# Second stage of a three-stage decoder kernel: the probability tiles are turned by VectorE in 32x32 blocks and eight DMAs, and the values come from two full-width products

## The reference

```
Q, K, V = split_heads(layernorm(x) @ W_Q), split_heads(ctx @ W_K), split_heads(ctx @ W_V)
E = einsum('bhqd,bhkd->bhqk', Q, K)            # one 64x64 block for each sequence and head
E = where(key_padding_mask, -inf, E)
A = softmax(E / sqrt(64))
x = x + einsum('bhqk,bhkd->bhqd', A, V).reshape(b, 64, 1024) @ W_O
```

## Time and profile before

| | |
|---|---|
| median of 3 runs | 3386.17 us (3384.32 to 3388.98) |
| profiled execution, span from first to last instruction | 3389.4 us |
| PE, DVE, ACT, POOL busy over the span | 98%, 82%, 83%, 73% |
| PE matmuls in one pass of stage two | 11.02 us busy of 11.15 us |
| DVE, ACT, POOL in the same pass | 5.12, 7.05, 3.10 us busy |
| second stage, first scores of tile 0 to last products of tile 31 | 194.4 to about 564 us |

### The profile page before, as it was taken

One profiled execution on the slowest core, in us unless ns is written; L12 is line 12 of the kernel. 1 busy time (PEld: TensorE's weight loads), 2 busy tenths in 40 slices (PEclk: granted clock), 3 DMA queues, 4 the chain that ended last, 5 costly groups with the idle time before them and its releaser, 6 DMA issues.

```text
span 3389.4 us, 120739 instructions
## 1 busy us (share of the span) xinstructions
PE 3317.7 (98%) x49605; PEld 2474.5 (73%) x49605; DVE 2767.5 (82%) x5297; ACT 2803.2 (83%) x5522; POOL 2483.0 (73%) x4812
## 2 busy tenths in 40 slices
PE   8989998999999999999999999999999999999997
PEld 6777876577777777777777777777777777777776
DVE  6844445888888888888888888888888888899995
ACT  5756665688888888888888888888888888888885
POOL 4622223888888888888888888888888888888884
PEclk8999999999999999999999999999999999999999
DMA  3000001544444444445444444444444444444441
GB/s 108 3 7 9 8 9 35 102 83 84 85 91 98 94 84 82 83 94 105 88 82 83 89 94 98 85 86 83 95 102 83 85 85 92 83 89 85 89 88 41
DMA packets 200381, 260.15 MB, mean 77 GB/s; under 512 B 123161, under 2 KB 145438, under 8 KB 199838
## 3 DMA queue, kind: packets, MB, share of 16 engines
q0 software_dynamic: 55296, 201.35, 31.4%
q1 hardware_dynamic: 143820, 50.88, 6.1%
q10 hardware_dynamic: 722, 0.21, 0.0%
HBM read 23.95 MB, written 2.10 MB: 8 GB/s over the span
## 4 chain that ended last, share of the span: by engine, by line
PE 95%; DVE 2%; POOL 1%; issue 1%; DMA 1%; ACT 1%; SPq 0%; DVEq 0%; POOLq 0%
PE bank L1059 19%; PE bank L1034 17%; PE bank L1110 10%; PE bank L1187 10%; PE bank L1158 8%; PE bank L1174 6%; PE bank L1129 5%; PE bank L1051 4%; PE bank L675 2%; PE bank L1124 2%; PE bank L688 2%; PE bank L697 2%; PE bank L752 2%; PE bank L367 1%; PE bank L660 1%; PE bank L377 1%
## 5 line engine op out<-in xcount | busy, mean ns | idle before, releaser
L1348 DVE TENSOR_TENSOR R<-bank,tables 128x1024 f32<-128x1024 f32 x768 | 904.7, 1220 | 174.7 <-ACT sq L1246 167.2
L1059 PE MATMUL bank<-WA,xcT 128*128 128x512 f32 x1536 | 723.6, 593 | 3.0 <-ACT xcT L1221 2.1
L1034 PEld LDWEIGHTS bank<-ident,R 128*128 128x128 f32 x3072 | 365.0, 141 | 214.7 <-issue 201.2
L1361 DVE TENSOR_REDUCE ss<-sq 128x16 f32<-128x1024 f32 x384 | 460.1, 1198 | 0.0
L1473 POOL TENSOR_TENSOR P<-P,inv_sum 128x512 f32<-128x512 f32 x384 | 447.6, 1331 | 2.9 <-DVE inv_sum L1402 2.9
L1246 ACT ACTIVATE sq<-bank 128x512 f32<-128x512 f32 x768 | 431.3, 587 | 16.0 <-PE bank L1059 16.0
L1034 PE MATMUL bank<-ident,R 128*128 128x128 f32 x3072 | 431.2, 273 | 8.8 <-POOL R L1461 6.8
L1461 POOL TENSOR_TENSOR R<-R,rn 128x512 f32<-128x512 f32 x384 | 400.4, 1043 | 31.5 <-DMA R<-R 5.4
L1467 POOL TENSOR_TENSOR P<-P,rn 128x512 f32<-128x512 f32 x384 | 402.6, 1048 | 4.3 <-DVE P L1390 4.3
L1059 PEld LDWEIGHTS bank<-WA,xcT 128*128 128x128 f32 x1536 | 262.2, 191 | 188.9 <-issue 184.0
L1187 PE MATMUL bank<-WO,OT 128*128 128x128 f32 x3072 | 374.6, 275 | 0.0
(11 more groups left out here) (154 smaller groups left out, 6857.6 us busy)
## 6 DMA issues: line engine op xcount, KB each, us to landing
R<-R POOLq DMA_DIRECT2D x384, 512.0 KB, 5.0
WA<-in_wqkv SPq DMA_DIRECT2D x24, 256.0 KB, 2.9
ystat<-Y SPq DMA_DIRECT2D x192, 32.0 KB
ystat<-Y SPq DMA_DIRECT2D x384, 15.8 KB
ys<-Y SPq DMA_DIRECT2D x192, 32.0 KB
ys<-Y SPq DMA_DIRECT2D x384, 15.8 KB
WV<-in_wqkv SPq DMA_DIRECT2D x6, 512.0 KB, 4.0
WO<-in_wo SPq DMA_DIRECT2D x6, 512.0 KB, 4.3
```

The source lines that it names most:

```text
L1034: return nc.tensor.transpose(dst, src, m.ident[:, :])
L1059: mm(b[QK_BANK[n, half]][:, :], m.xsT[:, t % 2, :], cols[:, half, :, :], start=True, stop=True)\
L1348: tt(both, src.unsqueeze(1).to_broadcast([128, 2, 16, 32]), tab.unsqueeze(2).to_broadcast([128, 2, 16, 32]), ALU.mult).then_inc(s.rotated. ...
L1361: nc.vector.tensor_reduce(m.ss[:, t % 2, 16 * n:16 * n + 16], m.sq[:, n, :].rearrange("p (h d) -> p h d", d=HD), AX.X, ALU.add)\
```

## The change

`probs_turned` moves from TensorE to VectorE. There, two `transpose` instructions a tile, one for each half of 512 columns, turn each 32x32 block in place within its group of 32 partitions and write it to `BLOCKS`, a part of the buffer `R` that only stage three uses otherwise. A block that must change its group of partitions is then moved by DMA: SyncE issues eight DMAs a tile from `BLOCKS` to `PT`, each from 32 partitions to 32 partitions, two runs of 1 KB on each partition (64 KB). `head_outputs` waits for all eight (semaphore `p_moved`, 128 a tile), and `probs_turned` waits for those of the tile before. ScalarE's two copies `probs_out` go. `PT` now has the keys of a sequence on one half of the partitions, so the values can stand by token: `values` makes two products of 128 tokens by 512 columns each. `outputs_out` writes `OT` in another order, and the wait for `y1` goes to `out_projection`.

```diff
+    BLOCKS = m.R[:, 0, 0, :].rearrange("p (a k n) -> p a k n", a=2, k=2)
+    PT = m.PT[:, :, :].rearrange("p t (a q n) -> p t a q n", a=2, q=2)
...
     @m.sync.append
     def _(sp):
+        def probs_moved(t):
+            if exists(t):
+                sp.wait_ge(s.p_turned[1], t + 1)
+                sp.wait_ge(s.p_turned[0], t + 1)
+                for to in range(4):
+                    for q in range(2):
+                        frm = to - to % 2 + q
+                        sp.dma_start(PT[32 * to:32 * to + 32, t % 2, :, q, :], BLOCKS[32 * frm:32 * frm + 32, :, to % 2, :])\
+                            .then_inc(s.p_moved[t % 2], 16)
...
         for t in range(N):
             at_least(sp, s.x_turned, t - 3)
             sp.dma_start(m.ctx_sb[:, t % 4, :], ctx_tiles[t, :, :]).then_inc(s.ctx[t % 4], 16)
+            probs_moved(t - 2)
+        for t in range(N - 2, N):
+            probs_moved(t)
...
         def out_projection(t):
             if exists(t):
                 pe.wait_ge(s.o_copied[0], t + 1)
                 pe.wait_ge(s.o_copied[1], t + 1)
+                at_least(pe, s.y1, t)
...
-        def probs_turned(t, j):
-            if exists(t):
-                pe.wait_ge(s.normal[j], t + 1)
-                if j == 1:
-                    at_least(pe, s.y1, t)
-                for n in range(4):
-                    at = j * 512 + n * 128
-                    last = turned(PT_BANK[j][:, n * 128:(n + 1) * 128], m.P[:, t % 2, at:at + 128])
-                last.then_inc(s.p_turned[j], 1)
...
         def head_outputs(t):
             if exists(t):
-                for j in range(2):
-                    pe.wait_ge(s.v_copied[j], t + 1)
-                    pe.wait_ge(s.p_copied[j], t + 1)
...
+                pe.wait_ge(s.v_copied[0], t + 1)
+                pe.wait_ge(s.v_copied[1], t + 1)
+                pe.wait_ge(s.p_moved[t % 2], 128 * (t // 2) + 128)
...
-        def values(t, bb):
-            if exists(t):
-                cols = WV.rearrange("p (j e n) -> p e j n", e=2, n=128)
-                for e in range(2):
-                    last = mm(V_BANK[bb][64 * e:64 * e + 64, :], m.ctxT[:, t % 2, bb * 64:bb * 64 + 64],
-                              cols[:, e, :, :], start=True, stop=True)
-                last.then_inc(s.v[bb], 1)
...
+        def values(t, j):
+            if exists(t):
+                mm(V_BANK[j][:, :], m.ctxT[:, t % 2, :], WV[:, j * 512:(j + 1) * 512], start=True, stop=True)\
+                    .then_inc(s.v[j], 1)
...
-            probs_turned(i - 1, 1)
-            probs_turned(i - 1, 0)
...
-            probs_out(i - 1, 1)
-            probs_out(i - 1, 0)
...
+        def probs_turned(t, a):
+            if exists(t):
+                dve.wait_ge(s.normal[a], t + 1)
+                at_least(dve, s.p_moved[(t - 1) % 2], 128 * ((t + 1) // 2))
+                blocks = m.P[:, t % 2, a * 512:(a + 1) * 512].rearrange("p (h k n) -> p k h n", k=2, n=32)
+                nc.vector.transpose(BLOCKS[:, a, :, :].rearrange("p k (h n) -> p k h n", n=32), blocks)\
+                    .then_inc(s.p_turned[a], 1)
...
             inverse_sums(i - 1, 1)
             inverse_sums(i - 1, 0)
+            probs_turned(i - 1, 1)
+            probs_turned(i - 1, 0)
             added(i - 2)
             less_maximum(i, 1)
             less_maximum(i, 0)
```

More of the change, by code:

```diff
@@ L624, in cross_attention @@
     S_BANK, QT_BANK, KT_BANK = (b[0], b[3]), (b[1], b[2]), (b[0], b[3])
-    V_BANK, PT_BANK, PV_BANK = (b[5], b[1]), (b[6], b[7]), (b[2], b[4])
+    V_BANK, PV_BANK = (b[5], b[1]), (b[2], b[4])
     OUT, TURNED_IN = b[7], b[4]
     WQ, WK, WV, WO = m.WA[:, 1, 0:INNER], m.WA[:, 1, INNER:2 * INNER], m.cross_wv, m.WO[:, 1, :]
+    BLOCKS = m.R[:, 0, 0, :].rearrange("p (a k n) -> p a k n", a=2, k=2)
+    PT = m.PT[:, :, :].rearrange("p t (a q n) -> p t a q n", a=2, q=2)
     def pair(name):
@@ L638, in cross_attention @@
     s.row_sum, s.inverse, s.normal = pair("row_sum"), pair("inverse"), pair("normal")
-    s.p_turned, s.p_copied = pair("p_turned"), pair("p_copied")
+    s.p_turned, s.p_moved = pair("p_turned"), pair("p_moved")
     s.o, s.o_copied, s.wo, s.y1 = sem("cross_o"), pair("o_copied"), sem("cross_wo"), sem("cross_y1")
@@ L672, in out_projection @@
                 pe.wait_ge(s.o_copied[1], t + 1)
+                at_least(pe, s.y1, t)
                 for c in range(PAIRS):
-                    at = (c % 2) * 512 + c // 2 * 128
-                    last = mm(OUT[:, 0:128], m.OT[:, t % 2, at:at + 128], WO[:, c * 128:(c + 1) * 128],
+                    last = mm(OUT[:, 0:128], m.OT[:, t % 2, c * 128:c * 128 + 128], WO[:, c * 128:(c + 1) * 128],
                               start=(c == 0), stop=(c == PAIRS - 1))
@@ L733, in head_outputs @@
             if exists(t):
-                for j in range(2):
-                    pe.wait_ge(s.v_copied[j], t + 1)
-                    pe.wait_ge(s.p_copied[j], t + 1)
[L737 to L746, removed]
-        def values(t, bb):
-            if exists(t):
-                cols = WV.rearrange("p (j e n) -> p e j n", e=2, n=128)
-                for e in range(2):
-                    last = mm(V_BANK[bb][64 * e:64 * e + 64, :], m.ctxT[:, t % 2, bb * 64:bb * 64 + 64],
-                              cols[:, e, :, :], start=True, stop=True)
-                last.then_inc(s.v[bb], 1)
+                pe.wait_ge(s.v_copied[0], t + 1)
+                pe.wait_ge(s.v_copied[1], t + 1)
+                pe.wait_ge(s.p_moved[t % 2], 128 * (t // 2) + 128)
+                for hp in range(PAIRS):
+                    for bb, a in ((0, 0), (1, 1), (0, 1), (1, 0)):
+                        rows, head, vals = slice(64 * bb, 64 * bb + 64), slice(64 * a, 64 * a + 64), (2 * hp + a) * 64
+                        last = mm(PV_BANK[bb][head, hp * 64:hp * 64 + 64], m.V[rows, t % 2, vals:vals + 64],
+                                  PT[rows, t % 2, a, :, hp * 32:hp * 32 + 32], start=True, stop=True)
+                        if hp == PAIRS - 1 and (bb, a) in ((0, 1), (1, 0)):
+                            last.then_inc(s.o, 1)
+        def values(t, j):
+            if exists(t):
+                mm(V_BANK[j][:, :], m.ctxT[:, t % 2, :], WV[:, j * 512:(j + 1) * 512], start=True, stop=True)\
+                    .then_inc(s.v[j], 1)
         for i in range(N + 2):
@@ L799, in exponents @@
                 nc.scalar.activation(part, part, ACT.Exp, scale=HD ** -0.5).then_inc(s.probs[a], 1)
-        def probs_out(t, j):
-            if exists(t):
-                act.wait_ge(s.p_turned[j], t + 1)
-                copy(m.PT[:, t % 2, j * 512:(j + 1) * 512], PT_BANK[j][:, :]).then_inc(s.p_copied[j], 1)
         def outputs_out(t, e):
@@ L808, in outputs_out @@
                 act.wait_ge(s.o, 2 * t + 2)
-                copy(m.OT[:, t % 2, e * 512:(e + 1) * 512], PV_BANK[e][:, :]).then_inc(s.o_copied[e], 1)
+                copy(m.OT[:, t % 2, :].rearrange("p (c b q) -> p b c q", b=2, q=SEQ)[:, e, :, :],
+                     PV_BANK[e][:, :].rearrange("p (c q) -> p c q", q=SEQ)).then_inc(s.o_copied[e], 1)
         def normalised(t):
```

## The result

| | before | after |
|---|---|---|
| median of 4 runs (lowest to highest) | 3387.43 us (3384.32 to 3388.98) | 3460.7 us (3456.55 to 3462.52) |
| ratio, 95% interval | | 1.0217 (1.0202 to 1.0231) |

What follows compares the result with a forecast made beforehand. PE's list was taken to bound the kernel, 11.16 us a tile. Ring 1 at 11.93 gave +23.1, first period -0.2, stage end +3.3, pauses about -1: together +25 on 3386.2, forecast 3411 us, range 3400 to 3446.

Steps and rivals of the forecast that it cites:

- Slower: Whole kernel: the change makes it slower by more than 0.2%, 6.8 us; chance 0.88.
- The transpose on VectorE: Each of VectorE's two transposes a tile takes 0.69 us, bounds 0.51 and 1.20.
- Ring 1: Stage two, scores through VectorE's transposes, `added`, `Y` and ScalarE's copies to the next scores: 11.93 us a tile.
- The moves: SyncE's eight DMAs: 0.56 us an issue, 1.8 landing, 5.88 from the last transpose to PE's head outputs.
- rival 2: The moves set stage two's period; at an issue interval of 0.76, 12.97 us a tile and 3445 us; chance 0.22.
- the first case: Ring 1 sets stage two's period, 11.8 to 12.2 us a tile, 3405 to 3421 us; chance 0.54.
- threshold of 0.61: SyncE's issue interval in us from which ring 2 becomes the longest ring.
- ring 2: Head outputs through `OT` copies, exponential, transposes and moves to the next head outputs: 11.57 us a tile.
- Ring 3: Loop through two tiles, W plus 12.63 us from scores to head outputs, halved: 11.78 us a tile.
- the sign that I had named for rival 2: PE waiting over 1 us at the head outputs would show the prediction wrong in favour of rival 2.
- W: PE's time from the start of head outputs to the end of the next scores, without transposes: 10.93 us.
- Values, `OT` writes, `PT` copies, SyncE's late loads: Full-width values, strided `OT` writes, dropped `PT` copies and later stage-three loads: each costed at nothing.

Runs made afterwards that it cites:

- no_turn: Kernel before without TensorE's eight transposes and ScalarE's two `PT` copies, nothing in their place, head outputs reading an old buffer: 3378.42 us, ratio 0.9979.
- moves_unread: Changed kernel with the eight moves sent to a spare buffer, PE waiting for them only before the last tile's head outputs: 3406.33 us, ratio 1.0065.
- one_move: Changed kernel with one DMA of 512 KB in place of the eight, no block changing its partitions: 3403.0 us, ratio 1.0054.
- ten_moves: Changed kernel with two further 64 KB moves to a spare place, for which PE waits too: 3499.36 us, ratio 1.0334.
- four_moves: Changed kernel with VectorE turning each half twice, so four moves are left, and `normalised` behind the last keys' copy: 3389.76 us, ratio 1.0012.
- two_queues: Changed kernel with four of the eight moves issued by GpSimd, four by SyncE, and `normalised` behind the last keys' copy: 3390.62 us, ratio 1.0014.
- values_full: Kernel before with its values made by two full-width products, nothing else changed: 3384.7 us, ratio 1.0002.
- kept_busy: Changed kernel with twelve identity transposes on PE between scores and head outputs, into an unread bank: 3444.81 us, ratio 1.0175.

## Why the prediction was wrong in size

- **Slower**: right, and the reason in part. PE's eight transposes hid the keys' copy and gave nothing a tile when they went: the period of no_turn is that of before, 11.16, where I had 0.23 us less. That its time is 7 us lower, which is 31 x 0.23, is luck: that gain does not lie in the period.
- **The transpose on VectorE**: 0.71, I took 0.69. The Trainium skill, "VectorE: DVE Perf Modes", section "The three transpose paths", led to an estimate of about 0.7, and the trace agrees.
- **Ring 1**: 11.93 worked out, 11.92 measured (moves_unread, one_move), by way of errors that cancel, so that the hit is part luck. In moves_unread the scores begin 0.35 after the last keys' copy ends, not 0.14, since the waits in front of them cost more than in tile 0. In return `added` begins 0.1 before the second transpose ends (at 327.82, that one at 327.90), and the last keys' copy begins 0.48 after the queries' in place of 0.57. Ring 1 is real but not the longest ring.
- **The moves**: this term failed, and with it rival 2 took the place of the first case. I took 0.56 for an issue and 1.8 for the landing; they are 0.64 and 2.0. The prediction's own threshold of 0.61 was passed. With these two the leg is 0.08 + 7 x 0.64 + 2.0 + 0.08 = 6.64 (measured 6.59 to 6.70), ring 2 is 12.33 (measured 12.40), and the prediction's formula gives 30 x 1.17 + 4 = +39, 3425 us, still in the range. Ring 3 has 12.3 with measured terms, (11.16 + 6.79 + 6.60)/2, where 6.79 is the time from the scores' end to the first issue (353.96 to 360.75); it too is above ring 1. ten_moves, one_move and four_moves show the size of one issue. PE waits over 1 us at the head outputs in 21 of 32 tiles, the sign that I had named for rival 2. So the failed step is the one that put both rings of the moves under ring 1. It alone leaves the time inside the range; what came with it, late landings and long rests, took it out: 3425 + 18.7 + 16.1 = 3460. The Trainium skill, "DMA: Bandwidth & Descriptors", section "Anatomy of one DMA", has about 50 ns for the sequencer's part on the software path; the rows show 0.54 for an issue of GpSimd's (two_queues), whose DMAs go through the software queue in the profile, and 0.60 for one of SyncE's, of which that section doesn't speak. The measurements decide.
- **Late landings**: 18.7 us that no term had. I had taken the landing as a constant, though the context's own row went up to 6.0.
- **PE's clock**: 12.5 us. Rival 2 had "some 10 us more" for it, and I left just that out of the range. A cost that comes only with a certain rival must be in the range with it.
- **W**: 10.93 is right only without the two `less` waits; with them it is 11.16. It had no part in the result, since W alone was not the bound.
- **Values, `OT` writes, `PT` copies, SyncE's late loads**: I cost them at nothing. values_full shows it of the first; no run shows the others apart.

## What to carry to other kernels

Where DMAs are to take the place of an engine's work on the path, price each issue of the queue in a row as its own step, and count issues before bytes: one DMA of 512 KB was hidden where eight of 64 KB cost over 50 us. Work that seems to fill an engine may only cover a wait; take it out alone before paying for its replacement. And look for waits that others imply: two of them cost some 8 us here, as much as this rebuild could win at best.

## What the runs showed of the hardware

**Issues.** On SyncE a move of 32 partitions by two runs costs 0.60 us and the next follows 0.04 later, whether a run has 1 KB or 512 bytes; one of 128 partitions and 512 KB costs 0.48. On GpSimd four took 2.22, 0.55 each, but GpSimd does nothing else meanwhile. With four on each queue at once a move landed after 2.6 to 2.7 us (medians), not 2.0.

**Late landings.** In twelve tiles the packets of the last move spread over 0.9 to 1.6 us in place of 0.4, and exactly there a packet of the queue for instructions (16 KB, 0.9 to 1.5 us on one of the 16 DMA engines) had begun before they were done. The DMA view of the leg that ends at 353.9, undisturbed, and of the one that ends at 368.4:

```profile
PT<-R SPq DMA_DIRECT2D x8, 64.0 KB, 2.0
```

```profile
q8 instruction: 1, 0.02, 1.1%
...
PT<-R SPq DMA_DIRECT2D x8, 64.0 KB, 2.1
```

The first view has no row of that queue. In kept_busy the same holds for 18 late landings; in four_moves no such packet began between the last issue and 1.6 us behind it, when that move's packets were about done, and no last move landed late. Four more tiles of after have such a packet while SyncE issues, and there the eight issues take 5.8 to 6.5 us; but in three others one runs then too, and the issues take 5.07. This cause rests on the coincidence alone; no run here moved the instruction fetches.

**PE's clock.** In after the granted clock fell behind, or within, each of the eleven pauses of 2.4 us or more in front of the head outputs. These took 1.28 to 1.99 us in place of 1.16 behind ten of them; at 313.71, after a pause of 2.51, they were still fast, but the values right behind them took 3.51 in place of 1.98:

```profile
313.71 1.16 PE L746 MATMUL bank<-PT,V 64*64 64x64 f32 x64 [2.51 <-DMA PT<-R]
314.80 3.51 PE L753 MATMUL bank<-V,xcT 128*128 128x512 f32 x4
```

From 315.2 to 318.4 us the granted clock was 0.50, the 1.2 GHz level. Of the shorter pauses four had the same, of 2.33, 2.00, 1.67 and 1.30 us; others up to 2.09 had not:

```profile
612.44 1.98 PE L746 MATMUL bank<-PT,V 64*64 64x64 f32 x64 [1.30 <-DMA PT<-R]
```

With one pause of 1.75 us in each pass (moves_unread) the clock stayed at 1.00 from 201 to 560 us. In after PE also pauses before the scores. What decides between pauses under 2.4 us stays open.

**Fulfilled waits.** Two semaphore waits that had been fulfilled long ago still cost PE 0.21 us, about 0.1 each, alike behind a wait that had just been released and where nothing was waited for.
